# Turning four instead of six of the first weight pieces on TensorE

## The reference, cut to what matters

```python
def ternary_quant(w_fp32, g=64):
    w = w_fp32.astype(bfloat16)
    w_g = w.reshape(-1, g)
    scale = clip(mean(abs(w_g), -1, keepdims=True), 1e-08, None)
    q = clip(round(w_g / scale), -1, 1)
    return (q * scale).reshape(w.shape)

def ffn(x):                                  # D = 512, H = 2048
    gate, up = split(x @ ternary_quant(w_gate_up).T, 2)
    return rms_norm(silu(gate) * up) @ ternary_quant(w_proj).T

x = x + 0.5 * ffn(layernorm(x))
x = x + attention(layernorm(x))
x = x + 0.5 * ffn(layernorm(x))
```

## Time and profile before

| what | value |
|---|---|
| median of 3 runs | 874.08 us (872.79 to 876.84) |
| the profiled execution | 873.84 us, span 871.2 us |
| PE busy | 852.2 us (98% of the span) |
| DVE busy | 511.7 us (59%) |
| ACT busy | 443.0 us (51%) |
| POOL busy | 71.5 us (8%) |
| mean granted TensorE clock | 0.996 |

### The profile page before, as it was taken

One profiled execution on the slowest core, in us unless ns is written; L12 is line 12 of the kernel. 1 busy time (PEld: TensorE's weight loads), 2 busy tenths in 40 slices (PEclk: granted clock), 3 DMA queues, 4 the chain that ended last, 5 costly groups with the idle time before them and its releaser, 6 DMA issues. The chain is left out here.

```text
span 871.2 us, 13142 instructions
## 1 busy us (share of the span) xinstructions
PE 852.2 (98%) x4932; PEld 413.3 (47%) x4998; DVE 511.7 (59%) x979; ACT 443.0 (51%) x822; POOL 71.5 (8%) x114
## 2 busy tenths in 40 slices
PE   6999999999999989999999999999999999999998
PEld 5544444444444434464646464444444444444445
DVE  7999997824347566657696958433443443432332
ACT  7976667536435555556657463543444344334331
POOL 2211001200010010000000000000000000000000
PEclk9999999999999999999999999999999999999999
DMA  9999508996747679960505062163433343333236
GB/s 262 179 182 125 76 1 169 216 223 185 163 117 149 112 147 196 185 125 1 86 1 86 1 147 97 21 113 73 73 73 72 73 73 73 73 73 61 61 69 136
DMA packets 257486, 94.70 MB, mean 109 GB/s; under 512 B 242832, under 2 KB 245648, under 8 KB 256400
## 3 DMA queue, kind: packets, MB, share of 16 engines
q1 hardware_dynamic: 248448, 73.42, 45.2%
q0 software_dynamic: 5024, 13.11, 6.7%
q10 hardware_dynamic: 3952, 7.34, 2.6%
HBM read 29.62 MB, written 8.39 MB: 44 GB/s over the span
## 5 line engine op out<-in xcount | busy, mean ns | idle before, releaser
L1643 PE MATMUL proj_ps<-down_w,slots 128*128 128x512 bf16 x910 | 202.9, 379 | 1.1 <-issue 0.2
L1172 DVE SCALAR_TENSOR_TENSOR slots<-up_ps,silu 128x512 f32<-128x512 f32 x117 | 80.9, 691 | 179.8 <-PE up_ps L1629 134.2
L1629 PE MATMUL gate_ps<-gu_w,xT 128*128 128x512 bf16 (+1 forms) x762 | 173.1, 368 | 3.1 <-ACT silu L809 2.3
L1629 PE MATMUL up_ps<-gu_w,xT 128*128 128x512 bf16 (+1 forms) x759 | 171.3, 366 | 0.9
L1643 PEld LDWEIGHTS proj_ps<-down_w,slots 128*128 128x128 f16 x928 | 90.7, 98 | 109.9 <-DVE xs L1194 0.8
L809 ACT ACTIVATE silu<-gate_ps 128x512 f32<-128x512 f32 x117 | 68.8, 588 | 142.9 <-PE gate_ps L1629 142.9
L819 ACT ACTIVATE o_buf<-slots 128x512 f32<-128x512 f32 x128 | 80.5, 629 | 113.7 <-DVE slots L1172 113.0
L1629 PEld LDWEIGHTS gate_ps<-gu_w,xT 128*128 128x128 f16 x776 | 74.0, 98 | 88.4 <-ACT silu L809 2.7
L1629 PEld LDWEIGHTS up_ps<-gu_w,xT 128*128 128x128 f16 x776 | 73.7, 98 | 84.4 <-issue 0.8
L1185 DVE SCALAR_TENSOR_TENSOR slots<-slots,inv 128x512 f16<-128x512 f32 x124 | 91.0, 744 | 3.7 <-ACT slots L830 3.6
L830 ACT ACTIVATE slots<-slots,inv 128x512 f16<-128x512 f32 x124 | 86.3, 711 | 11.1 <-POOL inv L709 7.6
(11 more groups left out here) (151 smaller groups left out, 942.4 us busy)
## 6 DMA issues: line engine op xcount, KB each, us to landing
gu_kept<-gu_w POOLq DMA_DIRECT2D x4, 1024.0 KB, 4.7
gu_w<-gu_kept POOLq DMA_DIRECT2D x4, 1024.0 KB, 6.2
out_dram<-xs SPq DMA_DIRECT2D x15, 256.0 KB, 2.4
xs<-in_L_attn_x_dram SPq DMA_DIRECT2D x3, 1024.0 KB, 8.5
aw<-in_L_attn_w_qkv_dram ACTq DMA_DIRECT2D x12, 256.0 KB, 2.9
slots<-in_L_ffn_w_gate_up_dram ACTq DMA_DIRECT2D x5, 512.0 KB, 6.7
aw<-in_L_ffn_w_gate_up_dram POOLq DMA_DIRECT2D x10, 256.0 KB, 5.5
aw<-in_L_ffn_w_proj_dram POOLq DMA_DIRECT2D x8, 256.0 KB, 5.5
```

What stands on the lines that cost most here:

```text
L1172: nc.vector.scalar_tensor_tensor(out=h_rows(i, q), in0=bank(up_ps, j), scalar=gu_out(i), in1=silu_rows(j), op0=ALU.mult, op1=ALU.mult).the ...
L1629: mm = nc.tensor.matmul(bank(ps, j)[:, first:first + width], xT(m)[:, t, r, k, :], gu_w[:, q, side, k, first:first + width], start=(k + r ...
L1643: mm = nc.tensor.matmul(proj_ps[:, use % 2, :], h_turned(i)[:, r, j, :], down_w[:, j, :], start=(r + j == 0), stop=(r == 1 and j == HC - 1))
```

## The change

The constant `PE_TURNED` goes from 6 to 4, and the wait in POOL's order that named `first_here[4]` outright names it through the constant (it is `first_here[PE_TURNED - 2]`, which is the same semaphore with 6).

```diff
-PE_TURNED = 6
+PE_TURNED = 4
...
             for t in range(TILES):
                 rstd(0, t)
-            pool.wait_ge(first_here[4], 16)
+            pool.wait_ge(first_here[PE_TURNED - 2], 16)
             load_piece(PE_TURNED)
             load_piece(PE_TURNED + 1)
             pool.wait_ge(x_here[1], 16)
```

## The result

The changed kernel takes 884.78 us (883.88 to 886.90, 4 runs) against 874.13 us before (872.79 to 876.84, 4 runs): +10.65 us, a ratio of 1.0119 with a 95% interval of 1.0082 to 1.0156. The profiled execution took 883.88 us, its span is 882.1 us. Single executions that a disturbance made 1.6 to 2.7 times as long are left out of every median in this text.

What follows compares the result with a forecast made beforehand. PE was taken to bound the kernel, through pair 8's start. Removed work 0 plus pair 8's 5.8 us delay (DVE's 3.9 plus 1.9) gave 879.8 us; range 875.5 to 885.

Steps and rivals of the forecast that it cites:

- the likeliest case: Pieces and transposes of the first 54 us come late as worked out: +5.8 us, own range 877 to 882, chance 0.58.
- the clock's rival: PE stands from 18.1 to 21.1 us and its clock halves: 4.0 us more, 883.9; clock or further stall, chance 0.12.
- What bounds the kernel: PE as a whole, busy 852.2 of 871.2 us; delay of pair 8, started at 54.65, delays the end by as much.
- Removing PE's sixteen transposes and ScalarE's signs: Work removed in a stretch that DVE sets: costed at 0; at most 2.1 us of PE and 2.2 of ACT.
- DVE's two more instructions: Two added `sign_bits` on DVE, an engine without a gap: 0.84 us, all on the path.
- Piece 3: Moved from ACT's queue to SP's, landing at 21.1, 3.1 us late; `least_scale(3)` 2.6 us late from this alone.
- The formula of the Trainium skill: One DMA takes about 2.0 us plus bytes at 436 GB/s, 3.2 for 512 KB; chain would give about 2.3 less.
- Piece 4 and DVE's wait: DVE stands from 22.46 to 25.5 us, 3.0 us, for piece 4's transpose, covering the 2.6 us of piece 3.
- D: How late DVE finishes piece 3 (27.35 before): 3.9 us, with bounds 0.84 and 5.4.
- The second stall: Pair 6 waits for tile 2 of x block 1, transposed behind piece 9: start at 53.1 us, before 46.35.
- the predicted chain: Pair 6's start summed as 38.1 + 3.9 + 5.5 + 1.3 + 3.3 + 1.0 = 53.1 us, the 3.9 being DVE's lateness.
- the 5.5 and 3.3 us: Terms for pair 6's start: 5.5 us for the load's usual landing, 3.3 us for tile 2's own transpose.

Runs made afterwards that it cites:

- The edit of one line in the kernel before: Kernel before, with only POOL's first two loads waiting for piece 2 instead of piece 4: 874.63 us, +1.6, ratio 1.0022.
- The four experiments on it: Changed kernel with piece 3 loaded by ScalarE: 884.90 us; signs of pieces 4, 5 by ScalarE: 883.45; both: 885.12; piece 3 by ScalarE, block 1's load later: 888.65.
- the signs taken by ScalarE: Changed kernel with the signs of pieces 4 and 5 taken by ScalarE from the turned bf16 piece: 883.45 us, +10.2, ratio 1.0114.
- The best median: Changed kernel with piece 3 by ScalarE, block 1's load behind transposes of 4 and 5, pieces 6 to 9 loaded sooner: 880.43 us, +6.5, ratio 1.0069.
- the kernel before with later loads: Kernel before, with POOL loading pieces 8 to 10 behind block 1's second, third and fourth rstd: 879.03 us, +5.1, ratio 1.0064.

## Why the prediction was near, and where it was off

The time lies in the predicted range, 0.2 us under its upper end, and outside the likeliest case's own 877 to 882. That it lies inside is in part luck: the upper end is that of the clock's rival, worked out with 4.0 us for the clock, of which 1.7 came in pair 6, and the rest of the way was made by terms of the likeliest case that were too small.

- **What bounds the kernel: right.** Pair 8's 9.7 us are nearly all of the loss, and are carried unchanged to 200 us; the 1.2 us behind were not foreseen. Removing PE's sixteen transposes and ScalarE's signs gave nothing that can be seen, though no run has that alone.
- **DVE's two more instructions: right in kind.** 0.34 us each from start to start, 0.7, where I wrote 0.84.
- **Piece 3: the term was mis-sized.** I took SP to reach its load 1.5 us sooner than the transfers behind it had, because POOL starts sooner. The step that failed is that "what queues behind them on SP gets through up to 1.87 sooner". POOL's sooner loads met block 0's transposes, and SP was held up to 17.79. The edit of one line in the kernel before shows that as the cause. There and in the changed kernel the load in this slot lands at 22.7, as it did before: the 1.5 us were worth nothing. Piece 3 was turned 4.7 us late, not 3.1. The formula of the Trainium skill that the prediction sets against the trace is given in its section for GpSimd's transfers; so of the two landings that it names only the 6.7 tests it, and the 7.5 is a transfer of SP's.
- **Piece 4 and DVE's wait: right in mechanism.** A gap ahead of the first sign bits, ended by a transpose, 3.85 us for 3.0. What I had not put into the sum is that the means of piece 3 end later than that wait: 0.83 us more, with PE's transposes of it at half clock (1.97 against 1.07). D was 5.4 instead of 3.9, at the upper bound that I had given. The four experiments on it show that the waits for pieces 3 and 4 cover each other, and that behind them stands the next one, for piece 6.
- **The second stall: the right queue.** The size of piece 9 ends the wait, not tile 2, which had landed at 54.74. With D = 5.4 the predicted chain gives 54.6 for pair 6, and it was 55.3. That is nearer than the working deserved: that piece 9's transpose moves its first packet only 2.6 us after its issue began is not in my sum by itself; the 5.5 and 3.3 us that I took from other places happened to hold nearly as much.
- **The clock: the rival came true in part.** I gave it 0.12 and 4.0 us. It was in fact granted at half twice. It cost 1.7 us in pair 6, and 0.9 in the turning of piece 3, which is already in D. Whether the 1.7 could be won back stays open. With the signs taken by ScalarE PE stood for 3.22 us ahead of pair 6 and the pair still ran at full clock, so the length of the stand alone did not decide it.

D +1.5, pair 6 +0.7, the clock +1.7: these 3.9 on the 5.8 of the sum are the 9.7.

What stays open: whether any order makes the kernel with four pieces as fast as the one before. The best median was +6.5, with single runs at 876.42; what parts 876.42 from 885.47 us I did not see, since only one of its runs has a trace. Open too is what adds the us behind pair 8. No kernel here beat the one before.

## What to carry to other kernels

When a work item changes its route, list for every slot of the written order which item is in it now, and compare its landing with its use; the work saved on the old route counts only if that engine sets the pace. Two waits that end at about the same time hide each other: undoing one shows little, and undoing both shows the next. Look for a stall's cost at the first work that every later step stands behind, here pair 8, and not in the time alone. Starting a transfer sooner can hold up another engine's: here POOL's loads, 1.9 us sooner, cost SP's queue 2.6 us.

## What the runs showed of the hardware

A DMA transpose of SP's queue issued at 48.81 moved its first packet after 51.4 us, while POOL's loads with conversion ran (630 packets of theirs to none of SP's from 48 to 51 us in the changed kernel); one of the kernel before with no such load beside it did after 1.2 us. POOL's loads, started 1.8 us sooner in the kernel before, made the issue of block 0's transposes on SP last until 17.5 instead of 15.1 us.

TensorE's granted clock went from 1.00 to 0.50 behind a stand of 2.37 us in the changed kernel (1.00 from 54 to 56 us, 0.50 from 57 to 59, 1.00 again from 60). It stayed at 1.00 behind stands of 2.50 us (the kernel before with later loads) and 3.22 us (signs by ScalarE) at the same place of the program.
